# A fused attention and expert layer on one core: a small bias loaded as a column, small weight loads issued by ScalarE, and a new hand-written order of all steps

## The reference, cut to what matters

```
q, k   = rope(ln(x) @ Wq.T), rope(ln(x) @ Wk.T)      # rounded to bfloat16
o      = sum over causal keys of exp(q.k / sqrt(128))  # one number a row
attn   = relu(o * fc1_w + fc1_b) @ fc2_w.T + fc2_b     # 16 inner values
x      = x + ln(attn)
h      = relu(ln(x) @ W1[1] + b1[1])                   # 256 hidden values
ffn    = h @ W2[1] + b2[1]                             # one expert has all the weight
x      = x + ln(ffn)
```

## Time and profile before

| | us |
|---|---|
| median of 3 runs | 91.46 (90.4 to 91.65) |
| the profiled execution, own time | 90.89 |
| its span, first to last instruction | 89.1 |
| PE busy in the span | 81.7 |
| DVE busy | 75.9 |
| ACT busy | 71.9 |
| POOL busy | 58.0 |

### The profile page before, as it was taken

One profiled execution on the slowest core, in us unless ns is written; L12 is line 12 of the kernel. 1 busy time (PEld: TensorE's weight loads), 2 busy tenths in 40 slices (PEclk: granted clock), 3 DMA queues, 4 the chain that ended last, 5 costly groups with the idle time before them and its releaser, 6 DMA issues.

```text
span 89.1 us, 1544 instructions
## 1 busy us (share of the span) xinstructions
PE 81.7 (92%) x449; PEld 50.0 (56%) x449; DVE 75.9 (85%) x223; ACT 71.9 (81%) x196; POOL 58.0 (65%) x70
## 2 busy tenths in 40 slices
...
GB/s 32 210 233 110 286 298 126 203 247 233 13 115 3 118 104 14 0 0 0 7 118 121 0 0 0 0 0 91 31 7 0 0 4 0 0 0 173 162 192 179
DMA packets 11852, 7.64 MB, mean 86 GB/s; under 512 B 819, under 2 KB 10948, under 8 KB 11844
## 3 DMA queue, kind: packets, MB, share of 16 engines
...
## 4 chain that ended last, share of the span: by engine, by line
PE 63%; ACT 12%; DVE 6%; DMA 5%; SPq 4%; POOL 4%; issue 1%; POOLq 1%; DVEq 0%
PE psum L716 21%; PE psum L763 15%; PE psum L730 13%; ACT psum L524 7%; PE psum L690 6%; DMA b_f<-b 5%; PE psum L752 5%; ACT qk L442 3%; POOL rstd L432 2%; SPq L301 2%; ACT cols_n L442 2%; DVE stats L501 1%; POOL rows_n L352 1%; DVE x L641 1%; PE psum L735 1%
## 5 line engine op out<-in xcount | busy, mean ns | idle before, releaser
L432 POOL TENSOR_TENSOR rstd<-mv,half_neg 128x4 f32<-128x4 f32 (+1 forms) x36 | 36.1, 1010 | 24.8 <-DVE mv L510 22.4
L524 ACT ACTIVATE psum<-psum 128x1024 f32<-128x1024 f32 (+7 forms) x48 | 36.7, 765 | 1.6 <-PE psum L730 1.3
L730 PE MATMUL psum<-rot 128*128 128x512 bf16 (+3 forms) x80 | 20.9, 348 | 0.0
L716 PE MATMUL psum<-cols_n,wqk 128*128 128x512 f32 (+1 forms) x36 | 17.0, 562 | 0.6 <-ACT cols_n L442 0.6
L716 PE MATMUL psum<-cols_n,w_c 128*128 128x512 f32 (+1 forms) x36 | 15.9, 551 | 0.0
L763 PE MATMUL psum<-w_c,hid 128*128 128x128 f32 x128 | 15.8, 276 | 0.0
L763 PEld LDWEIGHTS psum<-w_c,hid 128*128 128x128 f32 x128 | 15.0, 192 | 0.8 <-ACT hid L474 0.3
L730 PEld LDWEIGHTS psum<-rot 128*128 128x128 bf16 x80 | 7.0, 98 | 10.9 <-issue 5.2
L442 ACT ACTIVATE cols_n<-psum 128x512 f32<-128x512 f32 (+1 forms) x12 | 6.5, 542 | 5.4 <-PE psum L690 5.3
L641 DVE SCALAR_TENSOR_TENSOR x<-psum,rstd,x_s 128x128 f32<-128x128 f32 x32 | 9.0, 342 | 1.4 <-POOL rstd L432 1.3
L501 DVE BATCH_NORM_STATS2 stats<-psum 128x6 f32<-128x256 f32 x25 | 9.6, 421 | 0.4 <-PE psum L752 0.2
...
## 6 DMA issues: line engine op xcount, KB each, us to landing
...
rot<-qk SPq DMA_DIRECT2D x14, 128.0 KB, 2.4
...
x_s<-x SPq DMA_DIRECT2D x2, 128.0 KB, 2.4
table<-tables SPq DMA_DIRECT2D x2, 128.0 KB, 4.4
w_f<-w SPq DMA_DIRECT2D x2, 128.0 KB, 5.1
out<-x_s SPq DMA_DIRECT2D x2, 128.0 KB, 2.1
```

The source lines that it names most:

```text
L432: ready[k].done(eng.tensor_tensor(rstd[:, g, slot[k], t], mv[:, g, slot[k], t, 1], half_neg[:, 0:tiles], ALU.pow), n)
L524: exps.done(eng.activation(bank[:, 0:width], bank[:, 0:width], ACT.Exp, scale=scale_qk, accum_out=sums[:, g, s, j:j + 1]), n, j, s)
L716: made[name].done(eng.matmul(banks.of(name, n)[:, 0:tiles * P], weight, cols_n[:, g, c], start=True, stop=True), n)
L730: mm = eng.matmul(bank[:, at:at + width], query, qk_r[:, g0 + c, 1, 0:width], start=True, stop=c < gb)
```

## The change

The two DMAs of `load_fc` are issued by ScalarE and no longer by SP. `load_b2` reads b2 as a column, 128 elements of 4 bytes, and stands far later in SP's list. A new PE step `b2.0` multiplies that column, spread over 128 columns as the stationary operand, with `center`: this gives the centered bias on every partition, in a PSUM bank. A new DVE step `+b2.0.D` copies it to `b2_c`. ScalarE's `b2mean` and `b2` are gone. The whole list of steps has a new order, with other banks and with 32 steps on another engine than before. Three blanks fewer are in it (5 for 8).

```diff
-                    eng.dma_start(b2_f[:, :], b2[EXPERT:EXPERT + 1, :].to_broadcast([P, P])).then_inc(l_b2, 16)
+                    eng.dma_start(b2_f[:, :], b2[EXPERT].unsqueeze(1)).then_inc(l_b2, 16)
...
+            if name == "b2":
+                ins = copy(b2_c[:, :], banks.of(name, n)[:, 0:P])
...
 (block.scalar)
+                if name == "load_fc":
+                    eng.dma_start(fc_f[:, 2:2 + P], fc2_wb).then_inc(l_fc, 16)
+                    eng.dma_start(fc_f[:, 0:2], fc1_wb).then_inc(l_fc, 16)
...
-                elif name == "b2mean":
-                elif name == "b2":
...
-                    b2_done.wait(eng, 0)
+                    taken["b2"].wait(eng, 0)
...
 (block.tensor)
+                elif name == "b2":
+                    banks.free(eng, name, n)
+                    eng.wait_ge(s_center, 2)
+                    eng.wait_ge(l_b2, 16)
+                    made[name].done(eng.matmul(banks.of(name, n)[:, 0:P], b2_f[:, 0:1].to_broadcast([P, P]), center[:, :],
+                                               start=True, stop=True), n)
```

More of the change, by code:

```diff
@@ L45 @@
 STEPS = """
[L46 to L80, removed]
@@ new lines @@
+stat1.6 +tr1.3.A load_table.3 norm1.4.P +q.5.A stat1.7 scores.0.2.0@2 scores.0.3.0@7 +k.5.A scores.0.1.0@5 sin.2.D
+k.3@6 exp.0.3.0 swap.5 var1.6 var1.7 exp.0.1.0 rope.2.D tr1.4@0 exp.0.2.0 q.3@7 rstd1.7 cos.5.D load_b1.0 exp.0.0.0
++k.3.A load_b2.0 sum.0 scores.1.2.0@1 stat1.8 +tr1.4.A norm1.7.P scores.1.3.0@3 exp.1.2.0 +q.3.D hT.0@6 k.4@0 rstd1.6
+sin.5.D swap.3 +hT.0 scores.1.1.0@1 exp.1.3.0 rope.5.D fc2.0@5 norm1.6.P +k.4.D tr1.7@7 exp.1.1.0 scores.4.2.1@3
+part3.0.D scores.4.3.1@4 exp.4.2.1 q.4@0 var1.8 stat3.0.D +tr1.7.D exp.4.3.1 rstd3.0 scores.4.2.0@1 sin.3.D +q.4.A
@@ new lines @@
+tr1.6@7 exp.4.2.0 cos.3.D scores.1.0.0@3 swap.4 q.7@0 x1.0 cos.4.P exp.1.0.0 scores.4.0.1@1 k.7@2 +q.7.D exp.4.0.1
++tr1.6.A stat4.0 scores.4.1.0@3 +k.7.A scores.4.0.0@5 sum.1 exp.4.1.0 var4.0 scores.4.1.1@0 rope.3.D swap.7 k.6@1
+rstd4.0 cos.7.D exp.4.0.0 scores.2.2.0@2 hT.1@4 sin.4.D q.6@7 +hT.1 +k.6.D norm4.0.P scores.2.1.0@3 exp.2.2.0 w1.0@6
++q.6.D exp.4.1.1 scores.4.3.0@4 rstd1.8 sin.7.D exp.2.1.0 scores.2.3.0@2 swap.6 trz.0@7 exp.4.3.0 rope.7.D fc2.1@0
++w1.0.D norm1.8.P +trz.0.A b2.0@3 part3.1.D scores.6.1.1@4 exp.2.3.0 scores.2.0.0@6 h1.0@7 +b2.0.D exp.6.1.1 stat3.1.D
@@ new lines @@
+rope.4.D scores.6.3.1@2 rstd3.1 exp.2.0.0 +h1.0.D scores.3.3.0@4 exp.6.3.1 sum.2 h0.0@6 sum.4 cos.6.P x1.1 exp.3.3.0
+tr1.8@7 scores.6.2.0@2 +h0.0.D scores.6.0.1@0 stat4.1 exp.6.2.0 scores.3.1.0@4 y.0@6 sin.6.D exp.6.0.1 var4.1 +tr1.8.D
+rstd4.1 exp.3.1.0 rope.6.D hT.2@2 hT.4@3 scores.6.2.1@0 ybias.0 +hT.2 norm4.1.P scores.5.1.1@7 +hT.4 scores.6.3.0@4
+exp.6.2.1 part5.0.D fc2.4@2 stat5.0.D exp.5.1.1 rstd5.0 part3.4.D scores.6.1.0@0 exp.6.3.0 q.8@7 stat3.4.D out.0
+rstd3.4 exp.6.1.0 scores.5.2.1@5 k.8@4 +q.8.D exp.5.2.1 store.0 scores.6.0.0@0 x1.4 +k.8.A trz.1@7 exp.6.0.0
```

44 lines of the change are left out of this document (24 added, 20 removed).

## The result

The changed kernel is slower: 96.13 us median of 4 runs (95.69 to 96.77), against 91.56 for the kernel before in the same comparison (4 runs, 90.4 to 91.78). The ratio is 1.055, its 95% interval 1.043 to 1.067. Run again with other kernels, it gave 95.58, ratio 1.045 (1.036 to 1.053). The profiled run took 96.26, of which the span is 94.5: 5.4 more than before.

The account below looks back on a forecast made before the run. PE was taken as the one full engine, so time could be had mainly in the first 14 us. The terms sum to -0.94 from the 91.46 median, giving 90.5, range 89.2 to 92.4.

Parts of the forecast that it names:

- Part 3: Start of PE's work: the three blanks dropped ahead of fc have nothing on the path, 0.0.
- Part 2: SP's issue order at the start: wqk issued earlier, k of unit 1 at 6.7 for 7.20, -0.5; spread after it, +0.22.
- the clock rises later: Rival, PE's start: idle PE delays the rise to the upper clock; 92.8 halfway, 95.0 in full; chance 0.13.
- Part 6: Middle: ACT and DVE can follow a lead of about 1 us, +0.2 (0.0 to 0.4).
- Part 5: b2 returns as a PE matmul at some 32 us, two records, +0.22 (0.11 to 0.3).
- Part 7: Tail: two last-unit steps, `part5.7` and `stat5.7`, go from DVE to ACT, +0.06.
- Part 1: First 14 us: `b2mean` and `b2` leave ACT, closing PE's hole before q of unit 2, -0.74.
- Part 4: First 14 us: DVE waits less for unit 3's x, closing PE's rope holes, -0.2 (0.33 gain to 0.5 loss).
- the gap before `trz.0`: Middle: PE's wait there for POOL's `norm4.0` goes, with two more score steps ahead of it, -0.2.

Follow-up runs that it names:

- e1: Changed kernel with four blanks more, three ahead of the first transposes and one behind them; 92.77 us, ratio 1.011.
- e2: Kernel before without its group of three blanks ahead of fc; 93.28 us, ratio 1.011.
- g1: e1 with four long POOL operations (norm1 of units 6 and 7, cosine products of units 4 and 6) cut to a quarter; 90.58 us, ratio 0.998.
- h4: Changed kernel, its five blanks kept, with the four POOL cuts of g1; 94.59 us, ratio 1.022.
- h2: h1 with b2 as a column and a matmul, DVE's copy of it ahead of the sine product; 89.87 us, ratio 0.983.
- i1: Kernel before, old blanks, with only the b2 part (column and matmul), DVE's copy ahead of the sine product; 90.63 us, ratio 0.984.
- h1: Kernel before with one blank more in each group, five and four for four and three; 91.04 us, ratio 0.997.
- e4: Kernel before with only the fc loads issued by ACT instead of SP; 91.53 us, ratio 0.999.
- g2: Kernel before with the same four POOL cuts as g1, as a control; 91.16 us, ratio 0.995.
- g4: Kernel before, unchanged, run again for a second profile; 91.17 us, profiled run 92.06.
- g3: e1 with three q and k copies back on ACT and two other copies back on DVE, as before; 92.31 us, ratio 1.022.
- e3: Kernel before, order kept, with b2 as a column and a matmul, DVE's copy behind the sine product; 92.26 us, no usable ratio.
- i2: h2 with DVE's copy of b2 behind the sine product instead of ahead of it; 91.17 us, ratio 0.996.

## Why the prediction was wrong

Forecast 90.5, range 89.2 to 92.4; measured 96.13. Two steps failed, and both were costed close to nothing. Each cost more than the whole forecast gain of 0.94.

**Part 3 (three blanks fewer, 0.0) failed first.** It looked at what stood behind the blanks and found nothing on the path. Their effect was on the clock. With PE's hole at the start filled again by four blanks, e1 is 3.4 us faster; e2 shows that the kernel before pays as well when its three go (ratio 1.011, 1.9 us between the medians). The rest of the hole is from the new order of x loads, which part 2 priced by wqk alone: the x rows that PE's first transposes need land 1.2 us later than before (4.28 for 3.09). The rival "the clock rises later" was this mechanism, with the right decision point: the 256-column records of the changed kernel are 0.43 apart, and those of k of unit 1, at 8.76, 0.6. Its price in full was 95.0; the 1.1 us from there to the measured time are more than covered by part 6. It had a chance of 0.13, and the range left its far end out. The argument against it, that real work fills part of the hole, was the weak one: the two pairs of transposes stood behind 1.35 and 0.47 us of idle time. The Trainium skill (TensorE: Matmul & The Clock Gate, "The HAM clock gate") says that the throttled clock is the default and activity releases it. By that rule the direction is as measured, and the traces agree: the rise came at 5.0 in e1 and at 14.1 in the changed kernel.

**Part 6 (the middle, +0.2, bounds 0.0 to 0.4) failed second.** It added up the work of ACT and DVE with each instruction at its usual duration. It did not ask which POOL instruction would run beside which DVE instruction. The DVE instructions that lasted over 0.2 us longer than the median of their kind lost 3.4 us by it in the changed kernel (five of them) and 3.7 in e1 (five), against 0.4 before (one) and 0.8 in g1 (three). The traces give the price:

| | q of unit 5 starts | from there to the end |
|---|---|---|
| before | 13.86 | 75.2 |
| changed kernel | 17.15 | 77.3 |
| h3, the changed kernel again | 16.26 | 77.6 |
| h4, the same with shorter POOL work | 16.75 | 75.6 |
| e1, blanks back | 13.04 | 77.6 |
| g1, the same with shorter POOL work | 13.35 | 75.4 |

The first column is the clock's and the loads', the second the middle's. For the second, parts 5, 6 and 7 give +0.28 together. It measured +2.1 to +2.4 against before, and +0.2 to +0.4 once four POOL instructions are shorter: what was left out of the sum is this hold, and little else. The Trainium skill (SBUF — State Buffer, "SBUF: two separate sides") says that DVE and GpSimd share a port pair under an exclusive lock, which DVE instructions of certain kinds take, and that the other engine is then fully blocked. The traces agree for products and copies whose inputs lie in SBUF, beside POOL's `norm` and cosine instructions. In e1 the copy of `sum`, 0.22 in the kernel before, took 0.99, to within 0.1 of POOL's end. They don't agree for POOL's `rstd` of four columns: the copy of 0.22 before and the product of 0.68 at 28.51 ran beside one of 1.49 and one of 1.01 us at their usual length.

The rest of the sum held or missed by little:
- **Part 1** (-0.74) is right. Without `b2mean` on ACT the hole before q of unit 2 is gone in e1, h2 and i1. All that the b2 change carries (parts 1, 4 and 5, and the gap before `trz.0`) was forecast at -0.92, and h2 is 1.2 us under h1 by the medians and 0.9 between the traces.
- **Part 2** (-0.5, k of unit 1 at 6.7) is wrong in size. Wqk was issued at 2.26 and took 3.7 us to land, not 2.8, with three x loads ahead. With the clock repaired k of unit 1 starts at 7.27, no earlier than the 7.20 of before; the spread comes behind it, as forecast. Moving fc's issue costs and gives nothing (e4).
- **Part 4** (-0.2) holds: from `tr1.5` to q of unit 5 lie 1.34 us in e1 and 1.64 before, so 0.30 of the 0.33 are gone. i1 shows DVE's wait for x gone by b2's load alone, without the new order of x loads.
- **Part 5** (+0.22) is exact: two records, 0.22.
- **Part 7** (+0.06) is within 0.1: the tail is 6.0 long.

In e1 q of unit 5 is 0.82 ahead of before: that lead was there, where parts 1, 2 and 4 gave 1.22. With both failed steps undone (g1, which leaves POOL work out) the kernel stands at 90.58, 0.7 under the 91.25 of before in its comparison by the medians; its ratio of 0.998 is no gain clear of noise, and the cut POOL work may itself account for 0.1 to 0.5 (g2). So the forecast of -0.94 at the end was not met in any run of the new order.

What stays open: why the rise comes at about 5 or about 10 us in one and the same kernel (before and g4). In the eight traces of before, e1, g1, g2, g3, h1, h2 and i1 it came at 3.9 to 5.5; in g4, e3, e4 and i2, whose PE was as full, at 9.4 to 10.2. In the four traces in which PE waited for a load before 6 us for longer (0.75 us in e2, some 1.3 at a time in the changed kernel, h3 and h4) it came at 11.0 to 14.1. So such a wait went with a late rise each time, but more blanks did not buy an early one: i2 has h2's blanks and rose at 9.9. A variant of the changed kernel's order that keeps DVE's products off POOL's was not tried.
